# Routing of tile 1, two up products and early statistics moved within the attention batches

## The reference, cut to what is computed

```python
x = L0_attn_x                                     # 16 batches x 256 tokens x 128
x = x + _layernorm(attn(_layernorm(x)))           # 16 heads of 8, full softmax over 256 keys
x = x + _layernorm(ffn(_layernorm(x)))
# ffn, for each token: 32 experts of width 64, and a shared part of width 256
scores = sigmoid(x @ gate_w.T); sc = scores + e_bias
group_scores = top_k(sc.reshape(T, 8, 4), 2)[0].sum(-1)     # the best 4 of 8 groups stay
topk_idx = top_k(where(score_mask > 0, sc, 0), 6)[1]
topk_w = 2.5 * scores[topk_idx] / (sum + 1e-20)             # -> combine[T, 32]
h = square(relu(einsum('th,eih->tei', x, up_w))) * combine
out = einsum('tei,ehi->th', h, down_w) + square(relu(x @ shared_up_w.T)) @ shared_down_w.T
```

## Time and profile before

| | |
|---|---|
| median of 3 runs | 500.38 us |
| lowest, highest | 499.31, 500.88 us |
| the profiled execution | 500.0 us |
| its span in the profile | 498.2 us |
| mean granted TensorE clock | 0.974 |
| DMA, mean | 135 GB/s |

### The profile page before, as it was taken

How to read it: one execution, slowest core, us unless ns; L and a number is a source line. 1 busy time by engine, 2 the same in 40 slices (tenths; PEclk the granted TensorE clock), 3 DMA queues, 4 the chain that set the end, 5 groups by cost and what they waited for, 6 DMA issues and landing times.

```text
span 498.2 us, 10729 instructions
## 1 busy us (share of the span) xinstructions
PE 467.0 (94%) x3365; PEld 269.9 (54%) x3366; DVE 387.9 (78%) x1001; ACT 356.0 (71%) x707; POOL 248.5 (50%) x593
## 2 busy tenths in 40 slices
PE   6598999999999999998999899999999999999994
PEld 3233454554444445553456566666666666666662
DVE  4787888889899999889748788695968869496453
ACT  3415888888888878877676686868698776866551
POOL 7453233335666745427132627658393764626251
PEclk9777999999999999999899999999999999999999
DMA  8444444444444454420044254565453546445421
GB/s 234 145 120 156 131 126 115 136 140 136 138 135 145 133 151 141 137 67 3 3 171 132 80 186 137 165 185 176 115 206 95 165 148 191 175 121 202 132 102 42
DMA packets 49049, 67.48 MB, mean 135 GB/s; under 512 B 3808, under 2 KB 35808, under 8 KB 48992
## 3 DMA queue, kind: packets, MB, share of 16 engines
q1 hardware_dynamic: 48992, 66.78, 43.0%
HBM read 51.17 MB, written 15.20 MB: 133 GB/s over the span
## 4 chain that ended last, share of the span: by engine, by line
PE 72%; DVE 13%; issue 7%; DMA 3%; ACT 2%; POOL 1%; SPq 1%; POOLq 0%; DVEq 0%; ACTq 0%
PE pO L1330 9%; PE pY L1411 8%; PE pS L1411 8%; DVE mneg L986 8%; PE pS L1272 7%; PE pS L1395 6%; PE pS L1397 6%; PE pS L1396 6%; PE pS L1278 3%; DMA qk<-qk_scratch 2%; PE pY L1359 2%; PE pX L1257 2%; PE pY L1347 1%; PE pS L1442 1%; PE pX L1375 1%
## 5 line engine op out<-in xcount | busy, mean ns | idle before, releaser
L986 DVE TENSOR_REDUCE mneg<-pS 128x2 f32<-128x512 f32 x256 | 161.8, 684 | 23.9 <-PE pS L1272 21.5
L770 ACT ACTIVATE probs<-pS 128x512 f32<-128x512 f32 x256 | 141.3, 596 | 40.4 <-PE pS L1278 39.1
L1272 PE MATMUL pS<-qk 48*128 48x256 bf16 x512 | 87.9, 282 | 13.2 <-DMA qk<-qk_scratch 3.6
L855 ACT ACTIVATE h_ring<-r 128x512 f32<-128x512 f32 x104 | 64.3, 624 | 34.7 <-DVE r L1117 26.4
L1395 PE MATMUL pS<-qk,up_hi 128*128 128x512 f32 x144 | 88.4, 614 | 0.0
L1278 PE MATMUL pS<-qk 51*128 51x256 bf16 x512 | 85.3, 277 | 0.3 <-ACT probs L770 0.3
L1330 PE MATMUL pO<-probs,vv 128*32 128x256 f32 x1024 | 73.4, 395 | 0.0
L1272 PEld LDWEIGHTS pS<-qk 48*128 48x128 bf16 x512 | 34.4, 96 | 67.0 <-DVE mneg L986 35.2
L1117 DVE SCALAR_TENSOR_TENSOR r<-pS,probs 128x512 f32<-128x512 f32 x64 | 43.6, 689 | 27.3 <-PE pS L1397 26.4
L1397 PE MATMUL pS<-qk,up_lo 128*128 128x512 f32 x144 | 57.0, 396 | 0.0
L1396 PE MATMUL pS<-qk,up_hi 128*128 128x512 f32 x144 | 56.8, 394 | 0.0
(11 more groups left out here) (201 smaller groups left out, 830.3 us busy)
## 6 DMA issues: line engine op xcount, KB each, us to landing
c_ring<-c_scratch SPq DMA_DIRECT2D x32, 512.0 KB, 4.1
probs<-c_scratch SPq DMA_DIRECT2D x32, 512.0 KB, 4.1
qk<-qk_scratch SPq DMA_DIRECT2D x64, 192.0 KB
qk_scratch<-q_parts SPq DMA_DIRECT2D x16, 192.0 KB, 2.3
qk_scratch<-k_parts SPq DMA_DIRECT2D x16, 192.0 KB, 2.4
qk_scratch<-q_parts SPq DMA_DIRECT2D x16, 128.0 KB, 2.7
qk_scratch<-k_parts SPq DMA_DIRECT2D x16, 128.0 KB, 2.5
out_x<-probs SPq DMA_DIRECT2D x7, 256.0 KB, 4.6
```

The lines of the kernel that those rows point to most:

```text
L770: nc.scalar.activation(probs[j][:, hh], s2_bank(n)[:, :, :], ACT.Exp, scale=SCALE).then_inc(exp_done, 1)
L855: nc.scalar.activation(h_ring[:, (n - at) % HRING], r_sb[n % URING][:, :], ACT.Square).then_inc(sq_done, 1)
L986: nc.vector.tensor_reduce(mneg[u % 2][:, :, hh, k], pS1[n % S1_RING][:, :].rearrange("p (a s) -> p a s", a=TH), AX.X, ALU.max, negate=True ...
L1272: return mm(pS1[n % S1_RING][:, T * th:T * (th + 1)], qp[slot][rows, k, P * th:P * (th + 1)], kp[slot][rows, k, :], start=True, stop=True)
```

## The change

In batches 13 to 15 and tile 0:

- **Tile 0**: logits go from batch 13, pair 3 to pair 1, ahead of that pair's outputs; exp_logits from s = 7 to s = 3; route step 0 from (13, 12) to (13, 5). GpSimd starts the roots at unit 28 instead of 29, does all three root steps and the end at unit 29, and at unit 30 makes x's low part, which VectorE made at (14, 13). high_x(0) goes from (14, 4) to (14, 1). The first two up products go from batch 15, pairs 2 and 3, to batch 14, pairs 6 and 7; their rect from the first blocks of tile 0 to batch 15, s = 11 and 13.
- **Tile 1**: transpose_x1 goes from block 1 of tile 0 to batch 14, pair 2, keep_xT to s = 6; logits from block 2 to batch 14, pair 6, exp_logits to s = 14; route steps 0 to 4 to batch 15, s = 3 to 7. Steps 5, 6 and 7 stand at blocks 3, 4 and 6, transpose_c at block 9 instead of 13, root_score at block 1 instead of 5, root_of_sum after the first low part instead of the third. xT gets a second buffer. transpose_max(30) now waits for keep_xT(1), transpose_c(0) for exp_logits(1), and logits(1) no longer for keep_cT(0).
- **Statistics** of y and x1 for tiles 0 and 1: the four instructions in a row at s = 7 are spread over s = 6, 7, 11 and 12, in the same batches.

```diff
-ROUTE_AT = ((3, 4, 5, 6, 7, 8, 9, 11),
+ROUTE_AT = ((3, 4, 6),
             (1, 2, 3, 4, 5, 6, 7, 9))
-SPREAD_AT = (13, 11)
+SPREAD_AT = (9, 11)
+STATS_S = (6, 7, 11, 12)
+ROUTE_SECOND = (3, 4, 5, 6, 7)
+RECT_S = (11, 13)
-ROUTE_FIRST = {(NB - 3, 12): 0, (NB - 2, 11): 1, ...
+ROUTE_FIRST = {(NB - 3, 5): 0, (NB - 2, 11): 1, ...
-        xT = sb("xT", [P, TILE])
+        xT = [sb(f"xT{i}", [P, TILE]) for i in range(2)]
 # GpSimd, attention
+                if u == NU - 4:
+                    root_start()
                 if u == NU - 3:
-                    root_start()
                     root_step()
                     root_step()
-                if u == NU - 2:
                     root_step()
                     root_end()
+                if u == NU - 2:
+                    pool.wait_ge(xhi_done, 1)
+                    nc.gpsimd.tensor_tensor(x_lo[0], xT[0][:, :], x_hi[0].bitcast(F32), ALU.subtract).then_inc(xlo_done, 1)
 # GpSimd, tiles
                 low(i, 0)
+                if i == 0:
+                    root_of_sum(i + 1)
                 if i + 2 < NTILE:
                     residual1(i + 2)
...
-                if i + 1 < NTILE:
+                if 1 <= i < NTILE - 1:
                     root_of_sum(i + 1)
 # ScalarE
-                    if s == 4 and b == NB - 2:
+                    if s == 1 and b == NB - 2:
                         high_x(0)
+                    if s == 6 and b == NB - 2:
+                        keep_xT(1)
+                    if s == 14 and b == NB - 2:
+                        exp_logits(1)
-                    if s == 7 and b == NB - 3:
+                    if s == 3 and b == NB - 3:
                         exp_logits(0)
...
-                        if k == (5 if i == 0 else 3):
+                        if k == (1 if i == 0 else 3):
                             root_score(i + 1)
 # VectorE
-                    if b == NB - 2 and s == 13:
-                        low_x(0)
-                    if b in PREP and s == 7:
-                        stats_y(PREP.index(b))
-                    if b - 2 in PREP and s == 7:
-                        stats_x1(PREP.index(b - 2))
+                    if b in PREP and s in STATS_S:
+                        i = PREP.index(b)
+                        stats_early((y_kept, 2 * (i + 1)), ln2_done, stats2, ybig, y_stats, i, STATS_S.index(s))
+                    if b - 2 in PREP and s in STATS_S:
+                        i = PREP.index(b - 2)
+                        stats_early((x1_done, i + 1), ln3_done, stats3, xbig, x1_stats, i, STATS_S.index(s))
...
+                    if last and s in ROUTE_SECOND:
+                        if s == ROUTE_SECOND[0]:
+                            rt = Link(dve, rt_link, RT_LINKS)
+                        route(rt, 1, ROUTE_SECOND.index(s))
+                    if last and s in RECT_S:
+                        rect(0, RECT_S.index(s))
 # TensorE
-                    if last and j in (2, 3):
-                        pe.wait_ge(max_done, H * NB)
-                        up_block(0, j - 2)
+                    if j == 1 and b == NB - 3:
+                        pe.wait_ge(wb_loaded, 16 * N_WB)
+                        pe.wait_ge(mT_kept, 2 * b + 1)
+                        logits(0)
                     if j in (0, 1) and b >= 1:
                         for sh in range(TH):
                             outputs(b - 1, 2 + j, sh)
...
                         project_v(b + 1)
+                        if b == NB - 2:
+                            transpose_x1(1)
...
+                        elif b == NB - 2:
+                            pe.wait_ge(xT_kept, 2)
                         if last:
+                            pe.wait_ge(e_done, 2)
                             pe.wait_ge(mT_kept, NU)
                             transpose_c(0)
...
                             transpose_on(b - 1)
+                        if b == NB - 2:
+                            pe.wait_ge(mT_kept, NU - 1)
+                            logits(1)
+                    if j in (6, 7) and b == NB - 2:
+                        pe.wait_ge(max_done, H * NB)
+                        up_block(0, j - 6)
```

More of the change, by code:

```diff
@@ L805, in keep_xT @@
                 act.wait_ge(x2T_done, i + 1)
[L806 to L809, removed]
+                if i >= 2:
+                    act.wait_ge(logit_done, i - 1)
+                    act.wait_ge(xlo_done, i - 1)
+                copy(xT[i % 2][:, :], x1_bank(i)).then_inc(xT_kept, 1)
             def high_x(i):
@@ L814, in high_x @@
                     act.wait_ge(up_done, FBLK * (i - 1))
-                copy(x_hi[i % 2], xT[:, :]).then_inc(xhi_done, 1)
+                copy(x_hi[i % 2], xT[i % 2][:, :]).then_inc(xhi_done, 1)
             def high_up(c):
@@ L824, in exp_logits @@
                 if i >= 1:
-                    act.wait_ge(c_done, i)
+                    act.wait_ge(score_done, i)
                 nc.scalar.activation(e_sb[:, :, :], pX[:, 0:C4 * E], ACT.Exp, scale=-1.0).then_inc(e_done, 1)
@@ L928, in _ @@
                             keep_onT(NB - 1)
-                    if i == 0 and k == 1:
-                        keep_xT(1)
                     if i + 1 < NTILE:
-                        if k == (2 if i == 0 else 0):
+                        if k == 0 and i >= 1:
                             exp_logits(i + 1)
-                        if k == (5 if i == 0 else 3):
+                        if k == (1 if i == 0 else 3):
                             root_score(i + 1)
@@ L1015, in stats_y, with stats_early @@
                 ins.then_inc(y_stats, 1)
+            def stats_early(kept, used, to, tile, done, i, c):
+                if c == 0:
+                    dve.wait_ge(*kept)
+                    if i >= 1:
+                        dve.wait_ge(used, i)
+                ins = nc.vector.bn_stats(to[:, c, :], tile[:, C4 * i + c])
+                if c == C4 - 1:
+                    ins.then_inc(done, 1)
             def stats_x1(i):
@@ L1102, in low_x @@
                     dve.wait_ge(up_done, FBLK * (i - 1))
-                nc.vector.tensor_tensor(x_lo[i % 2], xT[:, :], x_hi[i % 2].bitcast(F32), ALU.subtract).then_inc(xlo_done, 1)
+                nc.vector.tensor_tensor(x_lo[i % 2], xT[i % 2][:, :], x_hi[i % 2].bitcast(F32), ALU.subtract).then_inc(xlo_done, 1)
             def rect(i, k):
@@ L1205, in _ @@
                     if i + 1 < NTILE and k in ROUTE_AT[i >= 1]:
-                        route(rt, i + 1, ROUTE_AT[i >= 1].index(k))
+                        route(rt, i + 1, ROUTE_AT[i >= 1].index(k) + (len(ROUTE_SECOND) if i == 0 else 0))
                     if i + 1 < NTILE and k == 12:
@@ L1371, in logits @@
                 pe.wait_ge(xT_kept, i + 1)
-                if i >= 1:
+                if i >= 2:
                     pe.wait_ge(cT_kept, i)
                 for c in range(C4):
-                    ins = mm(pX[:, E * c:E * (c + 1)], xT[:, P * c:P * (c + 1)], gate_sb[:, :],
+                    ins = mm(pX[:, E * c:E * (c + 1)], xT[i % 2][:, P * c:P * (c + 1)], gate_sb[:, :],
                              start=True, stop=True)
@@ L1441, in warm_up @@
                 for _ in range(n):
-                    mm(pS2[0][:, :, :].rearrange("p a b -> p (a b)"), xT[:, 0:P // 2].bitcast(BF16),
-                       xT[:, 0:T].bitcast(BF16), start=True, stop=True)
+                    mm(pS2[0][:, :, :].rearrange("p a b -> p (a b)"), xT[0][:, 0:P // 2].bitcast(BF16),
+                       xT[0][:, 0:T].bitcast(BF16), start=True, stop=True)
             pe.wait_ge(warm_set, 1)
@@ L1513, in _ @@
                             transpose_x1(0)
-                        elif b == NB - 3:
-                            pe.wait_ge(wb_loaded, 16 * N_WB)
-                            logits(0)
                     if j == 4:
@@ L1574, in _ @@
                     if i + 1 < NTILE:
-                        if i == 0 and k == 1:
-                            pe.wait_ge(cT_kept, 1)
-                            transpose_x1(1)
-                        if k == (2 if i == 0 else 0):
+                        if k == 0 and i >= 1:
                             logits(i + 1)
```

10 lines of the change are left out of this document (6 added, 4 removed).

## The result

The changed kernel takes 495.36 us (median of 8 runs, 491.59 to 496.64), beside it the kernel before 500.01 us (8 runs); the ratio is 0.9903, with a 95% interval of 0.9882 to 0.9925. So it is 4.6 us faster (3.8 to 5.9) where I had forecast 0.9 against the median and 1.3 against the profiled execution. Its profiled execution took 495.3 us with a span of 493.5.

What follows compares the result with a forecast made beforehand. TensorE, busy 94%, was taken as the bound, with VectorE setting the pace up to batch 14's last row maximum. Terms +0.5 - 0.2 - 0.5 + 1.5 - 0.5 - 2.1 = -1.3 gave 498.7, median 499.1 us, range 496.9 to 501.4.

Steps and rivals of the forecast that it cites:

- Statistics spread: Batches with statistics: VectorE is continuous from s = 3, so their place doesn't matter; 0 us, bounds -0.8 and +0.4.
- rival 4: Batch 15 shrinks by 1.8 us, or spread statistics return 0.6 us a batch: 1.6 to 2.4 less, about 497.2; chance 0.11.
- The forecast case: Whole kernel: the summed steps hold, giving 499.1 us as median, own range 498.0 to 500.2; chance 0.45.
- Batch 13: Earlier logits and route step 0 delay the maxima, so batch 14 starts later: +0.5 us, bounds -0.7 and +1.0.
- Batch 14: TensorE idle -0.2 us up to the last maximum, then -0.5 us as logits and up products fill waits.
- Batch 15: ScalarE's exponentials bind; of 1.8 us of up products moved out, 1.55 becomes idle: +1.5 us, bounds +1.0 and +1.8.
- Tile 0: Transposes, logits and their wait leave: -0.5 us idle; the 2.10 us stall at block 9 goes: -2.1, bounds -2.1 and -1.0.
- rival 3: Tile 0 keeps its stall, route step 5 at block 3 being held by h_lo: +2.1 us, 501.2; chance 0.07.
- rival 1: Batch 14's half-clock stretch goes, giving back up to 1.7 us, taken as 1.5: 497.6; chance 0.20.
- rival 2: TensorE starves and its clock falls in batch 13 or batch 15's pairs 2 to 4: 500.8, twice 502.5; chance 0.17.

Runs made afterwards that it cites:

- after once more: The changed kernel, unaltered, run again for a second profile; ratio to the kernel before 0.9889, batch 13 at 14.89 us.
- g1: Kernel before with tile 2's x1 statistics at block 9 of tile 0 instead of 7; project_y(14) to tile 1 41.22 us instead of 42.88.
- o1: Changed kernel with route step 0 back at (13, 12), roots at units 29 and 30, tile 0's logits still in pair 1; batch 13 took 14.60 us.
- c1: Changed kernel with the first two up products back in batch 15, pairs 2 and 3; ratio to the kernel before 0.9915.
- j1: Kernel before with root_score and its table load after block 7 of tile 0 instead of 5; project_y(14) to tile 1 41.88 us instead of 42.88.
- a1: Kernel before with only the statistics spread over s = 6, 7, 11 and 12; ratio to the kernel before 0.9975.
- e1: Changed kernel with all four statistics instructions at s = 12 to 15; ratio to the kernel before 0.9934.
- n1: Changed kernel with the statistics in a row at s = 7 again; ratio to the kernel before 0.9946.
- k1: Kernel before with 20 filler products of 128 columns added in pairs 3 and 4 of batch 14; ratio to the kernel before 0.9991.

## Why the prediction was wrong

At full clock in batches 13 and 14 on both sides (after once more against g1's batch 14) the change is worth 430.3 - 426.9 = 3.4 us: 431.7 of before less the 1.45 us of its fall. The prediction's working gave 1.3. By its steps:

- **Statistics spread: predicted 0, bounds -0.8 and +0.4; measured -1.5.** This is the step that failed, and it makes 1.5 of the 2.1 us between 1.3 and 3.4 (the misses of batches 13 and 14, 0.7 us each, cancel). The premise "VectorE is continuous from s = 3 on, so where they stand doesn't matter" leaves out its wait of some 0.57 us at the end of each batch. The earlier trace rows had a sign of it: in batch 6 VectorE was busy 12.00 of 13.30 us, and 0.8 us more of work made a batch only 0.6 us longer. A busy engine's delay isn't worth the same wherever it falls: early it delays TensorE, late it is met by a wait. It was half of rival 4, which had a chance of 0.11. The forecast case's own range, 498.0 to 500.2, isn't what the bounds of the steps add up to either; that is 496.2 to 502.0, and even so the measured 495.36 lies below it.
- **Batch 13: predicted +0.5, bounds -0.7 and +1.0; measured +1.16, and +2.7 where the clock falls.** The times that were worked out for VectorE came in: step 0 right after keep_v, then s = 6. But I took the delay at VectorE's s = 13. In VectorE's rows of the second trace it is continuous from norm_o to s = 1 of batch 14, and then waits 0.85 us:

```profile
223.41 0.36 DVE L1002 RECIPROCAL o_rec<-pY 128x32 f32<-128x32 f32 x1
...
224.15 5.15 DVE L996 TENSOR_REDUCE mneg<-pS 128x2 f32<-128x512 f32 x8
229.21 0.41 DVE L1013 TENSOR_TENSOR ybig<-pY,wvo_sb 128x256 f32<-128x256 f32 x1
230.48 1.29 DVE L996 TENSOR_REDUCE mneg<-pS 128x2 f32<-128x512 f32 x2 [0.85 <-PE pS L1299]
```

  In the kernel before step 0 at s = 12 was met by that wait (0.33 us left of it); now nothing late needs it. TensorE, held in pair 4 (waits of 0.36 and 0.84 us), had the rest of its own batch still before it, and 1.2 us of its 1.6 us of delay stayed (the second scores of pair 4 come 8.22 us into the batch instead of 6.61). By o1 the greater part of it, 0.87 us, hangs on the logits, which the prediction had hold up the maxima by 1.0 us and then met with slack of 0.48. The rows at the place itself, in the first trace:

```profile
217.01 1.29 DVE L996 TENSOR_REDUCE mneg<-pS 128x2 f32<-128x512 f32 x2 [1.33 <-PE pS L1299]
218.22 0.41 DVE L985 TENSOR_TENSOR vv<-pY,wvo_sb 128x256 f32<-128x256 f32 x1
218.55 0.22 DVE L1070 TENSOR_SCALAR score<-e_sb 128x128 f32<-128x128 f32 x1
218.80 0.95 DVE L1071 RECIPROCAL score<-score 128x128 f32<-128x128 f32 x1
219.78 2.48 DVE L996 TENSOR_REDUCE mneg<-pS 128x2 f32<-128x512 f32 x4
```

- **Batch 14: predicted -0.2 + 0.6 + 1.0 + 1.8 - 0.5 = +2.7 at an unchanged clock; measured 15.26 - 13.24 = +2.0.** The 0.61 us wait went and two others came, as forecast. Mis-sized is the idle time that the logits and up products fill: c1, with the logits but without the products, still has 0.8 us to fill at the end of batch 14, where I had counted 0.5 for both.
- **Batch 15: predicted -0.25, measured -0.24.** ScalarE binds there, as the earlier trace rows had it, and the waits are in pairs 2 to 4.
- **Tile 0: predicted -0.5 - 2.1 and 1.6 us of moved work, 4.2 in all; measured 42.88 - 38.39 = 4.5.** The chain by table load, residual and statistics of x1 is what g1 and j1 show. In the changed kernel VectorE still waits there, 1.67 us ahead of the statistics of x1, but these now start 1.3 us ahead of TensorE's project_y (266.55 and 267.88 us), where in the kernel before they start 0.4 us behind it (270.22 and 269.82), and no stall follows. Route step 5 took 0.29 us for comb, but h_lo began only behind it (260.34 and 260.60 us): rival 3 didn't come about, and what it would cost isn't shown. A further 0.3 us came in a later tile: from transpose_f(3) to transpose_f(4) the traces of before's layout take 29.37 to 29.43 us, those of the changed one 29.04 to 29.11. A weight load waits there for GpSimd's low part, 0.43 to 0.51 us in the traces of before's layout and 0.12 to 0.20 in the others; why GpSimd stands 0.3 us further behind TensorE in the kernel before stays open:

```profile
391.38 0.19 PEld L1421 LDWEIGHTS pS<-h_hi,down_hi 128*128 128x128 f32 x1 [0.46 <-POOL h_lo L645]
```

- **The low clock: rival 1 (it goes from batch 14) and rival 2 (it falls in batch 13) came both**, in the same execution, and in the second trace rival 1 alone. I had treated where the clock falls as a property of the kernel. It is one of an execution: of the traces of before's batch 14 (before twice, a1, g1, j1, all with the same waits) three fell and two did not; of those of the changed batch 13 (after twice, c1, e1, n1) two fell and three did not. So each kernel has such a loss in part of its executions, the kernel before also behind the stall of tile 0 (a1, k1), and the medians hold a mean over them.

What stays open is the rest between 3.4 us and the measured 4.6 (interval 3.8 to 5.9). Part of it, by the record, is the clock: the mean granted clock was 0.970 over the 54 executions of the kernel before that were measured beside the experiments, and 0.9745 over the twelve of the changed kernel. As an estimate, (1 - clock) x span / 0.5 makes that 30.1 and 25.2 us at half clock, 4.9 us less, which at 1.5 us for each 3.4 would be worth some 2 us. That is enough for the rest; but where in the execution those stretches lie isn't known without traces, and at the start one may cost less. The start may differ too, but its scatter of 4.9 us from trace to trace doesn't show it. The step that failed doesn't depend on this.

## What to carry to other kernels

Before saying that an engine is continuous and so the order of its work is free, look for its wait at the turn of the period: work placed so that only that engine is late there costs little (here 0.19 us for 0.68 us of work), the same work earlier makes the other engine late for good (0.57 us). A delay must be followed on both engines, past the point at which the first catches up. Work that comes earlier on one engine can also lengthen an instruction on another (j1). Where an engine's clock can fall after a thin stretch, compare several traces before putting that loss down to one kernel's order.

## What the runs showed of the hardware

- The granted clock fell to 0.50 for 3.4 us in one execution and not in another of the same program, after the same waits (batch 13: 16.40 and 14.89 us). Batch 14 of the kernel before shows it too, in programs that differ only behind it (14.69 us in before, 13.24 in g1). Each fall cost 1.45 to 1.5 us in a stretch in which TensorE is nearly always busy. In the one trace with fill products (k1) batch 14 kept its clock and tile 0 didn't, and over ten executions the time was that of before (0.9991); that the one led to the other isn't shown.
- A VectorE instruction of 0.18 us (picked_g) took 1.24 us in j1 while GpSimd's addition of 1.29 us ran, and one of 0.29 us (comb) took 1.34 us in the kernel before while GpSimd's h_lo of 1.28 us ran.
- The first 65 us scatter more than the rest does: the first project_y came between 63.0 and 67.9 us, from there on batches with the same code and waits repeat to some 0.02 us where the clock doesn't fall, but for the first one behind that point (13.33 to 13.56 us), and the tiles to 0.1 us.
